# Loads of a streaming graph layer: from the seventh row run of the second column group on, SP and ACT issue by turns

## The reference, cut to what matters

```python
h = jnp.maximum(_layernorm(x, axis=-1), 0.0)
neighbors = adj @ h
neighbors = neighbors / (num_neighbors[:, None] + 1e-7)
out = jnp.concatenate([h, neighbors], axis=-1) @ fc_w.T + fc_b
return x + jax.nn.relu(out)
```

## The kernel before, in words

| loads | group, runs | KB each | bytes per partition |
|---|---|---|---|
| 0 to 8, 9 | 0, runs 0 to 8, run 9 | 5120, 3840 | 40,960, 30,720 |
| 10 to 16 | 1, runs 0 to 6 | 4096 | 32,768 |
| 17 to 20 | 1, runs 7 and 8, two halves each | 2048 | 16,384 |
| 21 to 23 | 1, run 9, single rows | 1024 | 8,192 |
| 24 to 30 | 2, runs 0 to 6 | 784 | 6,272 |
| 31 to 34 | 2, runs 7 and 8, two halves each | 392 | 3,136 |
| 35 to 37 | 2, run 9, single rows | 196 | 1,568 |

## Time and profile before

### The profile page before, as it was taken

One profiled execution on the slowest core, in us unless ns is written; L12 is line 12 of the kernel. 1 busy time (PEld: TensorE's weight loads), 2 busy tenths in 40 slices (PEclk: granted clock), 3 DMA queues, 4 the chain that ended last, 5 costly groups with the idle time before them and its releaser, 6 DMA issues.

```text
span 245.8 us, 2444 instructions
## 1 busy us (share of the span) xinstructions
PE 207.6 (84%) x1084; PEld 86.0 (35%) x1084; DVE 41.3 (17%) x101; ACT 15.2 (6%) x35; POOL 4.2 (2%) x14
## 2 busy tenths in 40 slices
PE   0268689997879987999899899799997699798995
PEld 0143224342324433443344243234332233133662
DVE  1762033304300200050000530221000000002401
ACT  2130011201200110010000400000000000000000
POOL 6000000000000000000000000000000000000000
PEclk9999979999979999979999999899999999999999
DMA  9899999999999999999999999999999999999995
GB/s 305 381 440 447 440 441 424 427 427 435 414 433 428 433 423 427 427 427 422 443 440 427 427 424 423 432 437 437 424 432 427 411 427 424 421 420 418 424 403 211
DMA packets 7109, 102.79 MB, mean 418 GB/s; under 512 B 1364, under 2 KB 2172, under 8 KB 3900
## 3 DMA queue, kind: packets, MB, share of 16 engines
q1 hardware_dynamic: 6400, 102.37, 98.0%
q10 hardware_dynamic: 700, 0.28, 0.4%
HBM read 101.37 MB, written 1.28 MB: 418 GB/s over the span
## 4 chain that ended last, share of the span: by engine, by line
DMA 63%; PE 33%; SPq 2%; issue 0%; DVE 0%
DMA raw<-adj_group 63%; PE acc L612 28%; PE acc L631 2%; PE y L577 2%; PE turned L612 1%; SPq L249 1%; SPq L262 1%; PE y L646 0%; SPq L253 0%; PE y L644 0%; PE turned L565 0%; DVE out_sb L527 0%; PE acc L660 0%; SPq L258 0%; DVE sums L510 0%
## 5 line engine op out<-in xcount | busy, mean ns | idle before, releaser
L612 PE MATMUL acc<-raw,g_sb 128*64 128x512 f32 (+1 forms) x780 | 162.0, 570 | 21.5 <-DMA raw<-adj_group 21.5
L612 PEld LDWEIGHTS acc<-raw,g_sb 128*64 128x64 f32 x780 | 56.5, 141 | 121.8 <-issue 87.8
L612 PE MATMUL turned<-raw,g_sb 128*64 128x196 f32 x156 | 15.1, 336 | 1.3 <-DMA raw<-adj_group 1.1
L443 DVE TENSOR_TENSOR out_sb<-y,bias 128x128 f32<-128x128 f32 x20 | 4.4, 284 | 51.2 <-ACT g_sb L355 51.2
L577 PE MATMUL y<-w_both,ht 128*128 128x256 f32 (+1 forms) x40 | 12.1, 441 | 0.8 <-ACT ht L349 0.8
L612 PEld LDWEIGHTS turned<-raw,g_sb 128*64 128x64 f32 x156 | 10.2, 136 | 6.4 <-DMA raw<-adj_group 4.8
L493 DVE TENSOR_TENSOR sums<-acc,rnn_bc 128x512 f32<-128x512 f32 x4 | 2.6, 686 | 58.2 <-PE acc L612 56.2
L577 PEld LDWEIGHTS y<-w_both,ht 128*128 128x128 f32 x40 | 8.0, 217 | 3.9 <-issue 2.7
L519 DVE TENSOR_TENSOR out_sb<-y,out_sb 128x512 f32<-128x512 f32 (+1 forms) x5 | 3.2, 638 | 25.7 <-PE y L644 22.5
L565 PE MATMUL turned<-ident,h_pairs 128*128 128x128 f32 x20 | 3.7, 315 | 4.4 <-DVE h_pairs L431 4.4
L419 DVE TENSOR_REDUCE var<-sums 128x8 f32<-128x512 f32 x5 | 3.4, 687 | 21.5 <-ACT sums L329 21.5
(11 more groups left out here) (57 smaller groups left out, 44.9 us busy)
## 6 DMA issues: line engine op xcount, KB each, us to landing
raw<-adj_group SPq DMA_DIRECT2D x9, 5120.0 KB, 26.9
raw<-adj_group SPq DMA_DIRECT2D x7, 4096.0 KB, 28.4
raw<-adj_group SPq DMA_DIRECT2D x4, 2048.0 KB, 28.7
raw<-adj_group SPq DMA_DIRECT2D x7, 784.0 KB, 24.8
raw<-adj_group SPq DMA_DIRECT2D x1, 3840.0 KB, 24.4
raw<-adj_group SPq DMA_DIRECT2D x3, 1024.0 KB, 26.7
raw<-adj_group SPq DMA_DIRECT2D x4, 392.0 KB, 20.2
x_sb<-x SPq DMA_DIRECT2D x2, 576.0 KB, 4.7
```

The costliest lines, as they stand in the source:

```text
L443: last = nc.vector.tensor_tensor(to[:, 2 * k:2 * k + 2, :], weighed_parts(k, 0)[:, :, s, :], bias[:].unsqueeze(1).to_broadcast([LANES, 2, ...
L612: last = nc.tensor.matmul(acc[b][s * HALF:(s + 1) * HALF, 0:width], g_sb[:, t, :], raw[:, c + c0:c + c0 + width], start=g < G - 1 and t == ...
```

## The change

Load 17, the first half of run 7 of group 1, becomes the first of the part that two queues share (`TWO_QUEUES`). From there on SP issues every second load, 17, 19, 21 and so on to 37, and ACT issues 18, 20, 22 and so on to 36 on its own queue, after `load_rem(1)` and before its last store. That is 11 loads for SP and 10 for ACT. The function `load` is moved out of SP's program and takes the engine as an argument. Each load keeps its wait on `load_used`, its place in the ring, its semaphore and its shape; TensorE's order is unchanged.

```diff
+    TWO_QUEUES = [ld[:2] for ld in LOADS].index((1, FULL - 2))
+    assert (len(LOADS) - TWO_QUEUES) % 2
...
+        def load(engine, n):
+            g, m, i0, i1 = LOADS[n]
+            w = WIDTH[g]
+            if loads_before(n):
+                engine.wait_ge(load_used, loads_before(n))
+            r = RUN if m < FULL else TAIL_RUN
+            rows = adj_groups[g][m * BLOCK:m * BLOCK + r * LANES, 0:w].rearrange("(p i) c -> p (i c)", i=r)
+            engine.dma_start(raw[:, place(n):place_end(n)], rows[:, i0 * w:i1 * w]).then_inc(loaded(n)[0], 16)
...
-            for n in range(len(LOADS)):
-                load(n)
+            for n in range(TWO_QUEUES):
+                load(sp, n)
+            for n in range(TWO_QUEUES, len(LOADS), 2):
+                load(sp, n)
...
             load_rem(1)
+            for n in range(TWO_QUEUES + 1, len(LOADS), 2):
+                load(act, n)
             act.wait_ge(out_ready, LAST + 1)
```

More of the change, by code:

```diff
@@ L241, in _ @@
         def _(sp):
[L242 to L249, removed]
             def load_x(k):
```

## The result

The changed kernel takes 252.52 us (median of 6, 251.31 to 253.56) against 247.47 us for the kernel before (247.31 to 247.71): 5.05 us more, a ratio of 1.0202 [1.0177, 1.0227]. The profiled execution has a span of 251.0 us against 245.8.

What follows compares the result with a forecast made beforehand. The prediction took full DMA engines and the arrival order of queued loads as the bound, TensorE close behind. 3.3 us of later TensorE end plus 0.2 us of clock on 247.4 gave 250.9 us; narrow range 250.1 to 251.9, wide 249.1 to 253.1.

Steps and rivals of the forecast that it cites:

- (a): Engines share the queues another way: by bytes 251.7 to 252.6 us, or load by load 249.2 us; chances 0.12 and 0.12.
- (b): After the wait of over 6 us the clock stays at half through two stretches: 252.9 us; chance 0.1.
- What bounds the kernel: DMA engines never idle while loads are left; the order in which queued bytes arrive counts, with TensorE close behind.
- Steps 1 and 2: ACT's loads 18 and 20 alternate piece by piece with SP's queue: load 16 lands 8.0 us later, at 203.7.
- the count of 13 pieces: SP's pieces per engine still to come before load 16 lands, once ACT's first piece moves; taken between 12 and 14.
- The wait before load 15: TensorE's wait for load 15 grows from 2.02 us to some 4 to 5 us.
- Step 3: Load 17 lands at 212.0; TensorE ends load 16 at 210.7 and waits 1.3 us.
- Step 4: From load 17 on TensorE is the bound; its remaining work ends at 245.5, against 242.18 before.
- Step 5: TensorE's clock drops to half at loads 15 and 16, mostly hidden by waits; 0.4 us left, 0.2 us summed.
- The main store: At the kernel's end, issued at about 239.5 instead of 233.55, lands near 245, before the end; cost 0.
- No change: ACT's loads don't pass SP's queue, the engines serving what was issued first: 247.4 us; chance 0.06.
- faster: Two queues close what small pieces lose in group 2, ending 0.9 us earlier: 246.5 us; chance 0.04.

Runs made afterwards that it cites:

- experiment 1: The changed kernel, but ACT waits until load 16 has landed before it issues load 18: 247.93 us, ratio 1.0021 to the kernel before.
- experiment 4: The changed kernel, but TensorE takes the loads of group 1 in their order of arrival: 249.78 us, ratio 1.0098 to the kernel before.
- experiment 5: The changed kernel with six dummy matmuls before each of TensorE's waits for loads 15 and 16: 251.37 us, ratio 1.0164 to the kernel before.
- experiment 6: The changed kernel, but the two queues start at load 11 instead of 17: 255.00 us, ratio 1.0318 to the kernel before.

## Why the prediction was right, and what it sized wrong

It said slower, 250.9 us in a range of 249.1 to 253.1; 252.52 lies in it, and the mechanism is the one that the experiments show. But 5.05 us were lost where 3.5 were summed, and the forecast's own narrow range was missed (it is given as up to 251.9; its terms, 0.6 us for one piece more and 0.4 us of clock, give 251.7). The time lies in that part of the wide range that was there for rivals (a) and (b), and neither of them happened; so far the hit is luck.

- **What bounds the kernel:** right. The DMA share stays at 1.00 until the last loads are in at about 239 us, and order decides (experiments 1 and 4). That the engines run dry a little before 240 costs nothing, since TensorE waits for no load by then.
- **Steps 1 and 2, ACT's loads pass one piece for one:** the mechanism is right (209 against 208 packets, load 18 at 193.1 where "near 194" was said). The size is off: load 16 is 9.6 us late, not 8.0, and load 15 4.7 us, not 3 to 4. The term that failed is the count of 13 pieces, taken between 12 and 14. From ACT's first piece to 204.9 us ACT's queue moved 4.19 MB, which is 16 pieces of 16 KB per engine, as much as loads 18 and 20 together, and 16 x 0.61 = 9.8. Of the three pieces, the 2.5 us set aside for the landing, a figure without a row behind it, explain about one: without them the count is 13.9. ACT's start explains another: it is before 178.5 and not before 177.6, which makes it up to 18.1 / 1.23 = 14.7. The last piece or so stays open.
- **The wait before load 15:** 6.30 us, where 4 to 5 was given as the sign of the forecast. Its own terms, 2.02 us of before and 3 to 4 us of lateness, make 5 to 6.
- **The rule of the Trainium skill** (page "DMA: Bandwidth & Descriptors", section "Queues, rings and completion order"), by which an engine drains a packet of typically 9 to 17 descriptors before it switches: by it loads would alternate load by load and load 16 be 5 us late. The traces disagree with it, by the equal counts in the earlier trace rows and here, and by the 9.6 us.
- **Step 3, a gap of 1.3 us before load 17:** wrong in place. Load 16 ran at half clock until 209 and ended at 214.0 (205.3 + 6.9 + 1.8), after load 17 had landed (174.2 + 38.8 = 213.0, 1.0 us later than said), so TensorE was the bound from load 16 on. Without the half clock the gap is there, 0.57 us (experiment 5).
- **Step 4, TensorE's work after that:** right. From load 16 to the end it was 42.1 us; 6.9 + 33.4 for full clock, which experiment 6 shows as 40.3, plus 1.8.
- **Step 5, the clock:** the drop came at both places as said, the term was mis-sized: 0.2 us was put in, about 1 us was measured. With load 16 later than thought and load 17 not as much, the gap that should hide it was smaller than 1.3 us. (1.8 less 1.3 is also 0.5, not 0.4.)
- **The main store:** right; issued at 240.46 (239.5 was said), landed at 244.7, cost 0.
- **Rivals:** (a), sharing by bytes, 251.7 to 252.6 us, gives the right time, and even the right path (load 16 about 10 us late, no wait after it), by the wrong mechanism; the packet counts exclude it. (b), half clock through two stretches, did not come: the granted clock is 1.00 from 209.2 to 232. "No change" and "faster" are excluded by the measurement, and experiment 1 shows what "no change" would have needed: that nothing passes.

In the prediction's own terms the error is two terms of about 1 us each: load 17 landed at 213.0 and not 212.0, and the clock kept TensorE on load 16 for 1.0 us beyond that landing, where 0.2 us was put in.

The sum with measured sizes: 9.6 us of lateness, plus 1.8 of clock at load 16, less 6.1 us of waits that TensorE no longer has, is 5.3 us, against 247.42 - 242.18 = 5.2 us at TensorE's last matmul and 5.05 us in the medians. The 1.8 and the 6.1 both rest on the 40.3 us, which cancel in this sum. So it says how the loss divides and is no test of its size; the tests are the experiments.

## What to carry to other kernels

A second issuing queue is not only a way to issue: it is a second place in the line. In these runs a load put on the empty queue did not stand behind what the first queue held. It took turns with it piece by piece, and with a consumer that takes loads in a fixed order it delayed by its own bytes just what was needed first. Count what stands in the first queue at the moment of the first issue on the second, and compare the delay with the waits that the consumer still has left; the first 4.7 us here were free, the next 4.9 cost 5 us, about 1 us of it by the clock. Count too what stands ahead on the second queue, however small.

## What was not expected of the hardware

That turns go by pieces, whatever their size, was read from the earlier trace rows beforehand. What it does to small loads was not: two of them, 76 KB together, held load 12 back by 9 us, because a piece of 2 KB waits for a piece of 32 KB just as a large one does, and because, by the counts above, only about eight of the 16 engines carry them.
